# Attention and quantised FFN over 64 images: the row statistics of the second norm in the attention stage, both gelu tiles weighed on VectorE, and a new order of the FFN stage

## What is computed

```python
def rmsnorm(x, g):
    return x * jax.lax.rsqrt(jnp.mean(x * x, axis=-1, keepdims=True) + EPS) * g
def act_quant(x):
    scale = 127.0 / jnp.clip(jnp.max(jnp.abs(x), axis=-1, keepdims=True), 1e-05, None)
    return jnp.clip(jnp.round(x * scale), -128.0, 127.0) / scale
def bitlinear(x, w, g):            # w: weights rounded to -1, 0, 1
    xn = rmsnorm(x, g)
    return jnp.einsum('bsd,fd->bsf', act_quant(xn), weight_quant(w))
...
h = h + _L0_attn_ref(_layernorm(h, axis=-1), ...)
# _L0_ffn_ref(_layernorm(h)): bitlinear 192 -> 768, exact gelu, bitlinear 768 -> 192
h = h + _L0_ffn_ref(_layernorm(h, axis=-1), ...)
```

## Time and profile before

| | |
|---|---|
| median of 3 runs | 1894.72 us (1888.71 to 1895.52) |
| profiled execution: time, span | 1889.4 us, 1887.7 us |
| busy share of the span | PE 84%, DVE 72%, ACT 68%, POOL 58% |
| setup | to about 100 us |
| attention stage | to about 1360 us |
| FFN stage | 1360 us to the end |

### The profile page before, as it was taken

How to read it: one execution, slowest core, us unless ns; L and a number is a source line. 1 busy time by engine, 2 the same in 40 slices (tenths; PEclk the granted TensorE clock), 3 DMA queues, 4 the chain that set the end, 5 groups by cost and what they waited for, 6 DMA issues and landing times.

```text
span 1887.7 us, 50796 instructions
## 1 busy us (share of the span) xinstructions
PE 1579.8 (84%) x16574; PEld 1297.6 (69%) x16574; DVE 1364.8 (72%) x3151; ACT 1283.7 (68%) x1958; POOL 1089.7 (58%) x1503
## 2 busy tenths in 40 slices
PE   0539999999999999999999999999466666666666
PEld 0427788888888888888888888887345555555555
DVE  3636676767767676767676767676389999999996
ACT  1226666766767676767676666665288888888887
POOL 5035555555555555555555555554177777777775
PEclk9869999999999999999999999999666666666665
DMA  8674666665657565756565666660000000000000
GB/s 102 141 127 59 95 87 96 86 99 83 103 79 104 83 99 83 99 88 94 89 94 91 91 93 88 94 87 25 17 16 21 21 21 22 22 22 22 22 22 26
DMA packets 159967, 132.96 MB, mean 70 GB/s; under 512 B 32558, under 2 KB 151040, under 8 KB 159808
## 3 DMA queue, kind: packets, MB, share of 16 engines
q1 hardware_dynamic: 159168, 131.00, 44.4%
q0 software_dynamic: 768, 1.57, 0.5%
HBM read 118.32 MB, written 11.91 MB: 69 GB/s over the span
## 4 chain that ended last, share of the span: by engine, by line
PE 66%; DVE 15%; issue 7%; SPq 3%; ACT 3%; DMA 3%; POOL 1%; DVEq 1%; ACTq 0%; POOLq 0%
PE ps L1092 20%; PE ps L1176 8%; PE ps L1259 7%; PE ps L1250 7%; PE ps L1206 4%; DVE ff_st L860 4%; PE ps L1238 3%; PE ps L1232 3%; PE ps L1211 3%; PE ps L1336 2%; PE ps L1355 2%; DVE xpix L841 2%; PE ps L1167 2%; DVE xpix L853 1%; PE ps L1157 1%
## 5 line engine op out<-in xcount | busy, mean ns | idle before, releaser
L1092 PE MATMUL ps<-w_eff,pix 118*112 118x193 f32 (+1 forms) x2048 | 408.4, 337 | 25.0 <-ACT pix L909 24.3
L927 ACT ACTIVATE probs<-ps,isw 116x688 f32<-116x688 f32 x384 | 299.2, 831 | 171.6 <-PE ps L1238 171.6
L527 POOL TENSOR_TENSOR xpix<-probs,g_b 112x192 f32<-112x192 f32 (+1 forms) x512 | 296.5, 609 | 109.1 <-ACT probs L1044 99.7
L741 DVE TENSOR_REDUCE nmax<-ps 116x12 bf16<-116x1344 f32 (+2 forms) x192 | 299.6, 1560 | 80.2 <-PE ps L1211 77.7
L452 POOL TENSOR_TENSOR xsq<-xsq 118x784 f32<-118x784 f32 (+2 forms) x192 | 221.8, 1155 | 218.5 <-ACT xsq L920 208.4
L1092 PEld LDWEIGHTS ps<-w_eff,pix 118*112 118x112 f32 (+1 forms) x2048 | 309.8, 167 | 52.4 <-issue 18.9
L472 POOL TENSOR_SCALAR_AFFINE_SELECT probs<-probs 116x464 f32<-116x464 f32 x384 | 268.2, 717 | 46.5 <-ACT probs L927 31.0
L909 ACT ACTIVATE pix<-xpix 118x896 f32<-118x896 f32 (+1 forms) x128 | 198.4, 1552 | 104.9 <-DMA xpix<-in_x 56.0
L457 POOL TENSOR_TENSOR front_st<-front_st,expo 128x2 f32<-128x2 f32 x64 | 45.0, 703 | 235.2 <-DVE front_st L693 221.2
L1336 PE MATMUL ps<-w1t,xpix 96*112 96x384 f16 (+1 forms) x512 | 160.7, 488 | 14.6 <-ACT xpix L1035 13.3
L685 DVE TENSOR_SCALAR front_st<-ps 112x1 f32<-112x1 f32 (+1 forms) x128 | 18.3, 151 | 213.8 <-PE ps L1157 202.4
(11 more groups left out here) (161 smaller groups left out, 3363.3 us busy)
## 6 DMA issues: line engine op xcount, KB each, us to landing
xpix<-in_x SPq DMA_DIRECT2D x192, 196.0 KB
xpix<-in_x SPq DMA_DIRECT2D x192, 195.1 KB
rden<-den_rows SPq DMA_DIRECT2D x256, 85.5 KB, 2.1
out<-xpix SPq DMA_DIRECT2D x64, 87.0 KB
out<-xpix SPq DMA_DIRECT2D x64, 84.0 KB
xpix<-in_x SPq DMA_DIRECT2D x128, 34.1 KB
xpix<-in_x SPq DMA_DIRECT2D x128, 34.0 KB
den<-o_sb SPq DMA_DIRECT2D x256, 2.7 KB
```

Of the source, the lines that this page charges most:

```text
L527: last = nc.gpsimd.tensor_tensor(v2[0:P, b, tile, cols], gel[0:P, b, tile, cols], g2_b[0:P, cols], ALU.mult)
L741: V.tensor_reduce(dst, src, AX_X, ALU.max, negate=True).then_inc(s_mx, 1)
L927: A(probs[0:TB, g, 2 * e:2 * e + 2, :], ps[0:TB, 4 + 2 * e:6 + 2 * e, 0:SK], ACT.Exp, scale=isw[0:TB, 7:8]).then_inc(s_p, 1)
L1092: last = MM(ps_tok[tile][0:P, :], src, w_eff[0:HI, o, :], start=(o == 0), stop=(o == OFFS - 1))
```

## The change

- **Row statistics.** A new `measure(n - 1)` at the end of VectorE's attention step makes mean, variance, centred and weighed rows and their peaks for each image. GpSimd takes the inverse root in a new `row_roots(n - 2)`. Means, roots and peaks of all images are kept in small tables. Once, between the stages, five instructions over 128 columns turn them into the scales of the first quantiser for all images (`step1`, `scale1`).
- **FFN stage, VectorE.** Statistics and peak of the first quantiser are gone. Centring (`centre`) is repeated there, since the centred rows are not kept. VectorE multiplies both gelu tiles by g2 itself (`weigh`), a whole tile of 768 columns at a time, and forms the second quantiser's scales over 2 columns. `v1` lies in `tok_t`.
- **FFN stage, GpSimd** keeps only one addition and one power for each image (`gelu_roots`).
- **FFN stage, order.** TensorE: `turn_second(i - 2)`, `turn_first(i + 1)`, `ffn_first(i + 1)`, `ffn_second(i - 2)`. ScalarE: copy of the first transposes of image i+1, copy of the second transposes of image i-2, gelus and squares of image i+1, and last the quantising of image i-1, with a semaphore for each tile.

```diff
+            def row_roots(m):
+                pool.wait_ge(s_var2, m + 1)
+                nc.gpsimd.tensor_tensor(rms[:, bass.ds(m * 2, 2)], ln_st[:, 32:34], expo[:, 0:2],
+                                        ALU.pow).then_inc(s_rms, 1)
...
                 if old:
                     clear_later(n, 2)
+                if prev:
+                    row_roots(n - 2)
                 if newest:
                     add_squares(n + 3)
...
+            def gelu_roots(n, b):
+                after(pool, f_sc, n - 1)
+                pool.wait_ge(f_ssq, 2 * n + 2)
...
+                nc.gpsimd.tensor_scalar(ff_st[:, b, 18:20], gel_sum[:, b, :], EPS_RMS, None,
+                                        ALU.add).then_inc(f_var, 1)
+                pool.wait_ge(f_var, n + 1)
+                nc.gpsimd.tensor_tensor(ff_st[:, b, 20:22], ff_st[:, b, 18:20], expo[:, 0:2],
+                                        ALU.pow).then_inc(f_r1, 1)
...
+            def measure(n):
...
+                dve.wait_ge(s_h2, n + 1)
+                apart(dve)
+                for tile, P in enumerate((TA, TB)):
+                    last = V.bn_stats(ln_st[0:P, 20 + 6 * tile:26 + 6 * tile], h_all[0:P, hcols(n, tile)])
+                chain(last, 1)
+                apart(dve)
+                for tile, P in enumerate((TA, TB)):
+                    last = V.bn_aggr(ln_st[0:P, 34 + 2 * tile:36 + 2 * tile], ln_st[0:P, 20 + 6 * tile:26 + 6 * tile])
+                chain(last, 2)
+                after(dve, s_rms, n)
+                V.tensor_scalar(ln_st[:, 32:34], ln_st[:, 35:38:2], 1.0 + EPS_RMS,
+                                EPS_LN * EPS_RMS, ALU.mult, ALU.add).then_inc(s_var2, 1)
+                V.tensor_copy(mean2[:, bass.ds(n * 2, 2)], ln_st[:, 34:38:2])
+                for tile, P in enumerate((TA, TB)):
+                    last = V.scalar_tensor_tensor(v1[0:P, tile, :], h_all[0:P, hcols(n, tile)],
+                                                  ln_st[0:P, 34 + 2 * tile:35 + 2 * tile], g1_b[0:P, :],
+                                                  ALU.subtract, ALU.mult)
+                chain(last, 3)
+                for tile, P in enumerate((TA, TB)):
+                    last = V.tensor_reduce(peak[0:P, bass.ds(n * 2 + tile, 1)], v1[0:P, tile, :], AX_X, ALU.max,
+                                           apply_absolute_value=True)
+                last.then_inc(s_peak, 1)
...
                 if new:
                     maxima(n + 1, 2)
+                if prev:
+                    measure(n - 1)
...
+            link(V.tensor_tensor(peak[:, :], rms[:, :], peak[:, :], ALU.mult))
+            link(V.tensor_scalar(peak[:, :], peak[:, :], 1e-5, None, ALU.max))
+            link(V.reciprocal(inv_peak[:, :], peak[:, :]))
+            V.tensor_scalar(step1[:, :], peak[:, :], isw[:, 4:5], None, ALU.mult)
+            link(V.scalar_tensor_tensor(scale1[:, :], inv_peak[:, :], 127.0, rms[:, :], ALU.mult, ALU.mult))
+            dve.sem_inc(f_sc1, 1)
...
+            def weigh(n, b):
+                for tile, P in ((0, TA), (1, TB)):
+                    after(dve, f_q2[tile], n - 1)
+                    dve.wait_ge(f_g, 2 * n + tile + 1)
+                    V.tensor_tensor(v2[0:P, b, tile, :], gel[0:P, b, tile, :], g2_b[0:P, :],
+                                    ALU.mult).then_inc(f_v2[tile], 1)
...
+            def ffn_step(i, b, new=True, mid=True, last_=True):
+
                 if new:
...
+                    centre(i + 1)
+                    quantise_first(i + 1)
+                if last_:
+                    final(i - 3, 1 - b)
                 if mid:
...
+                    weigh(i - 1, 1 - b)
+                    peaks(i - 1, 1 - b)
+                    second_scales(i - 1, 1 - b)
...
+            def quantise(n, b):
+                act.wait_ge(f_sc, n + 1)
+                after(act, f_t2, n)
+                for tile, P in enumerate((TA, TB)):
+                    act.wait_ge(f_v2[tile], n + 1)
+                    A(q2[0:P, tile, :], v2[0:P, b, tile, :], ACT.Copy, bias=MAGIC16,
+                      scale=ff_st[0:P, b, 38 + tile:39 + tile]).then_inc(f_q2[tile], 1)
...
+            def gelus(m, b):
+                for tile in range(2):
+                    after(act, f_v2[tile], m - 1)
...
+            def ffn_step(i, b, new=True, mid=True, turned=True):
                 if new:
...
+                    copy_first(i + 1)
+                if turned:
+                    copy_second(i - 2)
+                if new:
+                    gelus(i + 1, 1 - b)
+                    gelu_squares(i + 1, 1 - b)
                 if mid:
...
+                    quantise(i - 1, 1 - b)
...
             def turn_second(n):
-                pe.wait_ge(f_q2, n + 1)
                 after(pe, f_t2s, n)
                 for tile, P in enumerate((TA, TB)):
+                    pe.wait_ge(f_q2[tile], n + 1)
...
+            def ffn_step(i, new=True, turned=True):
+                if turned:
+                    turn_second(i - 2)
                 if new:
                     turn_first(i + 1)
-                if last_:
+                    ffn_first(i + 1)
+                if turned:
                     ffn_second(i - 2)
-                if new:
-                    ffn_first(i + 1)
-                if mid:
-                    turn_second(i - 1)
```

266 lines of the change are left out of this document (115 added, 151 removed).

## The result

| | kernel before | changed kernel |
|---|---|---|
| median | 1893.51 us (1888.71 to 1895.52, 4 runs) | 1961.57 us (1955.1 to 1966.13, 4 runs) |
| profiled execution: time, span | 1889.4 us, 1887.7 us | 1959.77 us, 1958.0 us |
| ratio | | 1.0361, 95% interval 1.0324 to 1.0398 |

The change makes the kernel 3.6% slower. The page (busy tenths in 40 slices) answers to the earlier trace rows: VectorE fell from nine tenths to six or seven in the FFN stage, TensorE stands where it stood.

A forecast was written before the change was run, and what follows sets the result against it. Before, TensorE paced attention and VectorE the FFN stage; after, a ScalarE-TensorE round trip would set FFN steps. 1889.4 + 53 (steps) + 1 (start) + 2 (end) + 0 (attention) = 1945, put down as 1948 us; range 1912 to 1980.

The forecast's parts named there:

- Attention, 0 us: Attention stage: `measure`, 2.6 us, fits into VectorE's wait of 3.11 us a step, so the stage costs 0 us more.
- VectorE, 7.3 us and not the bound: FFN stage: VectorE's work sums to 6.66 us, 7.3 with idle share, below the forecast step of 8.85 us.
- rival B: FFN stage: VectorE's relief decides and the round trip is hidden; step 7.3 us, 1852 us, faster; chance 4%.
- Round trip, 1.57 and 1.08 us: FFN stage: ScalarE idles from quantising through TensorE's transposes to its next copy, 1.57 us at the lower clock, 1.08 at full.
- Step of 7.81 or 9.29 us by the clock: FFN stage: ScalarE's chain plus round trip, 7.81 us at full clock, 9.29 at lower; 30% full clock gives 8.85.
- Start, +1: Start of the FFN stage: scale instructions (0.9 us), centring and quantising on the path, +0.8 us, rounded to +1.
- End, +2: End of the FFN stage: from last copy of first transposes to end of span 25.1 us against 23.1, +2 us.
- A (full clock): FFN stage: TensorE stays at 2.4 GHz in most of it; step 7.81 to 8.3 us, 1882 to 1912 us; chance 12%.
- C (lower clock throughout): FFN stage: lower clock throughout, or added ScalarE cost; step 9.3 to 9.5 us, 1972 to 1990 us; chance 15%.
- D (attention): Attention stage: `measure` takes 3.3 us and overruns, +0.2 us for 60 steps, 12 us more, 1960 us; chance 7%.

## Why the prediction was right, step by step

The time (1961.57) lies in the range 1912 to 1980 and 14 us above the 1948 put down; the sign and the mechanism held. Against the sum of 1945 the profiled execution took 14.8 us more: 10.6 in the steps, 1.4 at the start, 2.3 at the end, and 0.4 that rounding the sum had left out. That the steps came so close is in part luck, as the two bullets on them say.

- **Attention, 0 us: right.** The wait of `front` fell from 3.11 us a step to 26.5 / 58 = 0.46, where 0.5 was said, the loads behind the last maxima wait what they waited, and GpSimd still has 2.6 us a step to wait. What this stage can show is limited by its scatter, some 8 us between kernels with the same program. Rows of 200 to 1280 us, answering to the earlier trace rows:

```profile
DVE front_st L691 <- PE ps L1209: 26.5, 58, 0.6
PEld ps L1258 <- DVE nmax L747: 19.3, 58, 0.3
POOL xsq L464 <- ACT xsq L963: 148.2, 58, 3.0
```

- **VectorE, 7.3 us and not the bound: right.** Its busy time is 275.28 / 400 of 9.03 us, 6.2 a step (6.66 summed; the products took 0.95 each, 0.97 said), and doubling the peaks moved nothing. GpSimd, which was to be under 20% busy, was at 27% (107.37 / 400), because its small additions are stretched, as shown at the end. The row taken for the interference before, L867, has a single input from SBUF and so does not bear on the rule named beside it; L911 in the run with the weighing on GpSimd has two, and takes 1457 ns against 161. The rule of the Trainium skill, "Perfetto Trace Analysis", section Identifying the Most-Contended Engine, led to rival B. Relieving VectorE did pay, 3.6% in the order of before, so the rule is not wrong about that engine; what it does not see is the loop between two others that came with the same edit.
- **Round trip, 1.57 and 1.08 us: mis-sized.** It took 1.31 and 0.86. The step that failed was to take the hand-over from the drain, where the transposes started 0.37 us behind the end of the quantising (1878.21 to 1878.58); in the loop the second tile's transposes start 0.05 us behind it (1602.29 + 1.75 = 1604.04, and 1604.09). The drain's hand-over did not stand alone: TensorE was still on the second layer's product (from 1876.62, 2.17 us) when the quantising ended, and the transposes stood behind it. One round earlier in the same trace TensorE waits for the quantising (1872.01 + 1.77 = 1873.78), starts its transposes 0.05 us behind it, and ScalarE idles 1.42 us, which with two transposes fewer is 1.24 at the lower clock, near the 1.31 measured. Rows of the kernel before:

```profile
1873.83 1.32 PE L1347 MATMUL ps<-ident_h,probs 112*128 112x112 f16 x12 [1.34 <-ACT probs L1023]
1875.19 1.37 ACT L1052 ACTIVATE xpix<-ps 128x672 f16<-128x672 f16 x2 [1.42 <-PE ps L1347]
1876.62 2.17 PE L1355 MATMUL ps<-w2t,xpix 128*112 128x192 f16 x12 [1.46 <-ACT xpix L1052]
```

- **Step of 7.81 or 9.29 us by the clock: lengths nearly right, mixture wrong.** 7.58 and 9.18 are the lengths that the runs show. The full-clock one was too long by the round trip alone. The other has two errors that partly cancel: the round trip 0.26 too long, and the gelus' wait 0.17 too short, since on image 0 the first gelu starts 2.22 us behind the copy and in the step above 2.39 (1607.74 - 1605.35). But I weighted the two by the granted clock's time share, 30%. The share fell to 22%, and, more important, the changed kernel has no step of 7.58: in all 60 the first layer's product, for which the gelus wait, took 2.80 us, the lower clock (1606.09 in the step above), while the first transposes ran at the lower clock in 43 and at the full one in 17. With the lengths measured the same 30% would have given 8.70 us, 0.33 under the 9.03; the lengths put down too long gave 0.15 of that back by luck, and 0.18 us a step is left. A share of time is no share of steps; the rows needed were those of the product itself.
- **Start, +1: measured +2.4.** The term that was mis-sized is the scales for all images. Five instructions over 128 columns were taken at the price of small ones, 0.9 us; from L844's start to the end of L848 it is 2.06 us, and the reciprocal alone is 0.95. A further 0.8 us, within the scatter of the attention stage, is that the last attention residual came at 1360.31 instead of 1359.53.

```profile
1363.68 0.29 DVE L844 TENSOR_TENSOR peak<-rms,peak 128x128 f32<-128x128 f32 x1
1364.27 0.95 DVE L846 RECIPROCAL inv_peak<-peak 128x128 f32<-128x128 f32 x1
1365.46 0.28 DVE L848 SCALAR_TENSOR_TENSOR scale<-inv_peak,rms 128x128 f32<-128x128 f32 x1
1365.90 0.75 DVE L863 SCALAR_TENSOR_TENSOR tok_t<-h_all,mean,g_b 112x192 f32<-112x192 f32 x2 [0.16 <-DVE scale L848]
```

- **End, +2: measured +4.3.** I had the scales ahead of the quantising by 4 us and so left VectorE out of the drain. There the final rows of image i-3 wait for TensorE and stand ahead of the weighing; so the scales came late for the last two quantisings. That VectorE's scales would hold back the quantising was named as a sign of being wrong; it came true here and in no step of the windows above. Rows, against the earlier trace rows:

```profile
1940.80 1.76 ACT L1065 ACTIVATE probs<-xpix,ff_st 112x768 f16<-112x768 f32 x2 [0.60 <-DVE ff_st L909]
1947.61 1.76 ACT L1065 ACTIVATE probs<-xpix,ff_st 112x768 f16<-112x768 f32 x2 [2.65 <-DVE ff_st L909]
```

- **Rivals.** A (full clock) is refuted by 0.61, and its price was too high: with the round trip at the full clock 60 steps of 7.58 would have made it 1889.4 - 23.4 + 3 = 1869. C (lower clock throughout) was right for the product that the gelus wait for, and its step was too long (9.3 to 9.5 against 9.18 in 34 steps). D (attention) did not occur, and the longer measure shows that its price was too high: there an overrun of 0.54 us a step cost 5 to 14 us over the stage, where 0.2 us was to cost 12.

## What to carry to other kernels

When two engines hand work to each other in fixed orders, follow each queue around the loop: if engine X's last item releases Y's first and Y's second releases X's next, the hand-over is paid in every step, however idle everybody is, and one item that nobody waits for, put behind X's hand-over, hides it (here 1.65 us of squares). Test a change of several parts part by part: here two parts gained 3.6% and a third lost 7.5%, and one part had either sign depending on whether another was there. Where a step has a length for each clock, count steps by the work that was slow in them, not by the mean clock.
